# A two-layer CIN kernel: 64x32 tiles with single fields as weights meet 230 streaming products, in place of product rows that meet single fields

## The reference, cut to what matters

```python
B, M, D = 512, 39, 64                      # r_x: (512, 39, 64); W0: (39, 39, 128); W1: (39, 128, 128)
x0 = h = x
for W in (W0, W1):
    h = einsum('bid,bjd,ijh->bhd', x0, h, W)
    outs.append(h)
out = concatenate(outs, axis=1).sum(axis=-1)   # (512, 256)
```

## Time and profile before

| | |
|---|---|
| runs of the kernel | 349.57, 349.65, 349.71 us; median 349.65 |
| profiled execution, span from the first to the last instruction | 348.3 us (the profile holds no other time of this execution; the runs lie 1.3 us above the span) |
| setup, up to the first sums of the main loop | 0 to 104.8 us |
| main loop | 104.8 to 346 us |
| last copy and store | 2.3 us |
| busy share of PE, DVE, ACT, POOL | 94%, 49%, 33%, 3% |

### The profile page before, as it was taken

The page is one execution under the profiler, slowest core; times in us unless marked ns, Lnnn a source line. Parts: engine busy times, 40 slices in busy tenths (PEclk is TensorE's granted clock), DMA queues, the critical chain, the costliest instruction groups (busy, mean ns, idle before and its releaser), DMA issues.

```text
span 348.3 us, 11398 instructions
## 1 busy us (share of the span) xinstructions
PE 329.0 (94%) x5397; PEld 292.8 (84%) x5397; DVE 171.4 (49%) x212; ACT 114.7 (33%) x210; POOL 10.1 (3%) x14
## 2 busy tenths in 40 slices
PE   0899997999889999999999999999999999999997
PEld 0566664555779999998999999899999999999996
DVE  2205469467899385444536572635358090812000
ACT  1366653343542243060306214230522332142300
POOL 9200000000000000000000000000000000000000
PEclk9999999899999999999999999999999999999999
DMA  7950431300040003700000090000006000000000
GB/s 301 385 117 2 155 146 32 122 1 0 2 154 4 2 2 77 229 4 2 19 2 2 13 274 25 0 19 2 4 3 154 2 2 17 4 2 4 4 0 15
DMA packets 4350, 20.03 MB, mean 58 GB/s; under 512 B 592, under 2 KB 1104, under 8 KB 3920
## 3 DMA queue, kind: packets, MB, share of 16 engines
q1 hardware_dynamic: 3728, 18.79, 16.8%
q10 hardware_dynamic: 576, 0.52, 0.5%
HBM read 18.78 MB, written 0.52 MB: 55 GB/s over the span
## 4 chain that ended last, share of the span: by engine, by line
PE 90%; DVE 6%; DMA 1%; ACT 1%; issue 0%; SPq 0%; DVEq 0%
PE out_ps L545 37%; PE stage L511 32%; PE stage L473 8%; PE stage L487 7%; PE stage L493 4%; PE stage L476 2%; DVE arena L354 2%; DMA arena<-in_w_rows 1%; DVE arena L287 1%; DVE arena L400 1%; DVE arena L362 1%; DVE arena L359 1%; DVE arena L375 0%; ACT arena L423 0%; DVE arena L323 0%
## 5 line engine op out<-in xcount | busy, mean ns | idle before, releaser
L545 PE MATMUL out_ps<-arena 114*128 114x128 f32 (+2 forms) x968 | 128.7, 294 | 0.5 <-ACT arena L440 0.5
L511 PE MATMUL stage<-arena 128*60 128x80 f32 (+4 forms) x4096 | 126.2, 227 | 3.1 <-DVE arena L354 2.1
L511 PEld LDWEIGHTS stage<-arena 128*50 128x50 f32 (+2 forms) x4096 | 123.8, 128 | 5.3 <-issue 3.3
L545 PEld LDWEIGHTS out_ps<-arena 114*128 114x128 f32 (+1 forms) x968 | 121.7, 192 | 5.8 <-ACT arena L440 0.6
L440 ACT COPY arena<-stage 114x480 f32<-114x480 f32 (+4 forms) x136 | 72.5, 540 | 138.9 <-PE stage L511 138.9
L354 DVE TENSOR_TENSOR arena<-arena 128x3200 f32<-128x3200 f32 x16 | 55.7, 3486 | 28.4 <-PE stage L511 28.3
L473 PE MATMUL stage<-arena 128*128 128x380 f32 (+1 forms) x78 | 34.3, 523 | 10.1 <-DVE arena L289 10.1
L487 PE MATMUL stage<-arena 128*114 128x512 f32 (+1 forms) x60 | 31.5, 608 | 3.1 <-DVE arena L375 3.1
L357 DVE TENSOR_TENSOR arena<-arena 128x640 f32<-128x640 f32 x16 | 13.2, 824 | 39.2 <-PE stage L511 39.2
L362 DVE TENSOR_TENSOR arena<-arena 128x800 f32<-128x800 f32 x32 | 30.2, 985 | 0.0
L414 ACT COPY arena<-stage 128x480 f32<-128x480 f32 (+1 forms) x39 | 22.1, 568 | 22.5 <-PE stage L476 22.5
(11 more groups left out here) (22 smaller groups left out, 43.5 us busy)
## 6 DMA issues: line engine op xcount, KB each, us to landing
arena<-in_x_dense SPq DMA_DIRECT2D x8, 640.0 KB, 7.0
arena<-in_x_single SPq DMA_DIRECT2D x16, 320.0 KB, 5.0
arena<-in_c_first SPq DMA_DIRECT2D x1, 2560.0 KB, 9.1
arena<-in_w SPq DMA_DIRECT2D x2, 640.0 KB, 7.0
arena<-in_c_second SPq DMA_DIRECT2D x1, 1280.0 KB, 6.4
arena<-in_w SPq DMA_DIRECT2D x1, 1216.0 KB, 9.8
arena<-in_w_square SPq DMA_DIRECT2D x1, 800.0 KB, 4.3
arena<-in_c_one SPq DMA_DIRECT2D x2, 256.0 KB, 10.1
```

Of the source, the lines that this page charges most:

```text
L511: done = nc.tensor.matmul(bank[PART * part:PART * part + r1 - r0, 0:count * 2 * some] .rearrange("p (i b) -> p b i", b=2 * some)[:, 2 * (t ...
L545: done = nc.tensor.matmul(to, sums, w, start=tile == 0 and s == 0, stop=last, skip_group_check=True)
```

## The change

Setup and main loop are written anew; the mathematics is the same.

**Lists and tiles.** The products of a pair are now two lists of 230 (with field pairs of the first and of the second half of the fields, some copies of single fields for the remaining terms, and some extra pairs). They are the *streaming* operand. The stationary operand is 32 single fields (`ROWS`), of one sample: 64 rows by 32 columns of PE. A pair needs four such matmuls, sample (rows `r`) by list (`which`); even and odd pairs go to different halves of PE's columns (`odd`), so that 8 tiles of 64x32 take turns. No zeros are streamed. The two samples go to two PSUM banks; each list is cut in two halves of 115 `SLOTS`.

**ACT** empties a group of four pairs with four copies of 64 partitions and 460 elements (`L379`); half of them write to the other 64 partitions than they read.

**Weighing.** Eight batches of 32 pairs. 115 slots of all 128 rows, each with 64 samples as stationary columns and 128 columns of C, in turn in the two column halves, then 11 + 4 matmuls for the first layer's output; a quarter of it follows each unit of 8 pairs. ACT and DVE add the two halves at the end of a batch. The 4 use rows of the sums that SP gathers by DMA.

**POOL** copies the single fields among the products (two copies per unit).

**Setup.** 32 matmuls of 512 columns (`DIRECT`) give the part of C that W1 and the W0 of the pair give directly, with slots on the partitions. ACT copies each to SBUF and SP turns it with four DMAs from SBUF to SBUF: each reads 90 to 115 partitions, 512 bytes of each, and writes them in a row into *one* partition of `c0`. `c_landed` counts all 128. The rest of C comes from 845 matmuls of 32x128 (`mixed`, L420) in 29 PSUM banks, which DVE adds to `c0` (L345) once everything has landed. The first four units' products and sums lie between (`PRODUCTS_BEHIND`, `SUMS_BEHIND`).

The core of the diff:

```diff
-FIELDS = 39
-ONE = 39
+ROWS = 32
+ROW0 = (8, 0)
+LIST = 230
+SLOTS = 115
...
-    PAIRS = 64
-    HALF_PAIRS = PAIRS // 2
+    PAIRS = 32
+    UNIT = 8
+    GROUP = 4
+    B = 2 * PAIRS
...
+        DIRECT = [(g, which, q) for g in range(PLACES // 4) for which in range(2) for q in range(2)
+                  if 4 * g >= ROW0[which] and 4 * g + 4 <= ROW0[which] + ROWS]
...
+        COUPLES = [4, 6, 0]
+        def couple(g):
+            return g % 2 if g < BATCH_GROUPS else g % 3
+        SUMS_BEHIND = {16: 0, 20: 1, 24: 2, 28: 3}
+        PRODUCTS_BEHIND = {7: 0, 10: 1, 13: 2, 16: 3}
...
+        def _(pool):
+            nc.gpsimd.memset(view(c0, (1, ZEROED * HID)), 0.0).then_inc(c_zeroed, 1)
+            for u in range(UNITS):
+                x, to = x0 + u % X_RING * XU, prod0 + u % PROD_RING * PROD + LIST
+                pool.wait_ge(x_loaded[u % X_RING], 16 * (u // X_RING + 1))
+                if u < PROD_RING:
+                    pool.wait_ge(c_landed, C_LANDED)
+                    pool.wait_ge(out1_ready, 2)
+                else:
+                    pool.wait_ge(filled, 2 * (u - PROD_RING + 1))
+                T, TO = (X_WORDS, UNIT), (2 * LIST, UNIT)
+                nc.gpsimd.tensor_copy(view(to, TO, (1, COPY0)), view(x + X_MAIN + 21, T, (1, COPY0)))
+                nc.gpsimd.tensor_copy(view(to + SLOTS, TO, (1, COPY1)), view(x + X_MAIN + 29, T, (1, COPY1)))\
+                    .then_inc(copies_ready, 1)
...
+            for i, (g, which, q) in enumerate(DIRECT):
+                sp.wait_ge(direct_copied, i + 1)
+                j = direct_slots(g, which, q)
+                c = 2 * q + which
+                row = ROWS * c + 4 * g - ROW0[which]
+                for f in range(4):
+                    sp.dma_start(view(c0 + j * HID, (HID, SLOTS - j), (1, HID), rows=(row + f, row + f + 1)),
+                                 view(d0[c] + (4 * g - ROW0[which] + f) * HID, (1, HID), rows=(j, SLOTS)))\
+                        .then_inc(c_landed, 16)
...
+            def gather(n):
+                sp.wait_ge(emptied, BATCH_GROUPS * (n + 1))
...
+                for c in range(4):
+                    row = ROWS * c + ONE - ROW0[c % 2]
+                    sp.dma_start(view(t2_0 + (4 * (n % 2) + c) * B, (1, B), rows=(0, SLOTS)),
+                                 view(s0[n % 2], (B, SLOTS), (1, B), rows=(row, row + 1))).then_inc(t2_moved[n % 2], 16)
...
+            def products(u):
+                x, to = x0 + u % X_RING * XU, prod0 + u % PROD_RING * PROD
+                dve.wait_ge(x_loaded[u % X_RING], 16 * (u // X_RING + 1))
+                if u >= PROD_RING:
+                    dve.wait_ge(filled, 2 * (u - PROD_RING + 1))
+                T, TO = (X_WORDS, UNIT), (2 * LIST, UNIT)
+                second = to + LIST
+                main, half = x + X_MAIN, x + X_MAIN + 21
+                mult(view(to + 20, TO, (10, 20), (1, 10)), view(main, T, (1, 20), (0, 10)),
+                     view(x, T, (1, 20), (1, 10)), ALU.mult)
...
+                mult(view(second + 130, TO, (10, 10), (1, 10)), view(half + 9, T, (1, 10), (0, 10)),
+                     view(half + 9, T, (1, 10), (1, 10)), ALU.mult).then_inc(prod_ready, 1)
...
+            dve.wait_ge(c_landed, C_LANDED)
+            for k in range(MIXED):
+                words = min(IN_BANK, SLOTS - IN_BANK * k) * HID
+                c = view(c0 + k * BANK, (1, words))
+                dve.wait_ge(mixed_filled, k + 1)
+                add(c, c, bank_view(mixed_bank(k) * BANK, (1, words)), ALU.add).then_inc(c_added, 1)
+                if k in PRODUCTS_BEHIND:
+                    products(PRODUCTS_BEHIND[k])
...
+            act.wait_ge(c_landed, C_LANDED)
+            act.wait_ge(v_ready, 1)
+            for g in range(GROUPS):
+                n, in_batch = divmod(g, BATCH_GROUPS)
+                at = COUPLES[couple(g)] * BANK
+                act.wait_ge(filled, g + 1)
+                for odd in range(2):
+                    for q in range(2):
+                        done = nc.scalar.copy(
+                            view(s0[n % 2] + 8 * in_batch + 2 * odd, (1, 2), (B, SLOTS), (4, 2),
+                                 rows=(HALF * q, HALF * q + HALF)),
+                            bank_view(at + 2 * SLOTS * q, (BANK, 2), (2, SLOTS), (1, 2),
+                                      rows=(HALF * odd, HALF * odd + HALF)))
+                done.then_inc(emptied, 1)
...
+                nc.tensor.matmul(bank_view(i % DIRECT_BANKS * BANK, (1, 4 * HID), rows=(0, SLOTS)),
+                                 view(u0 + which * LIST + q * SLOTS, (1, SLOTS)),
+                                 view(w1_0 + 4 * g * HID, (1, 4 * HID)), start=True, stop=True).then_inc(direct_filled, 1)
+            def mixed(k):
+                bank = mixed_bank(k)
+                if k < 8:
+                    pe.wait_ge(direct_copied, len(DIRECT) - DIRECT_BANKS + k + 1)
+                else:
+                    pe.wait_ge(c_added, k - 8 + 1 if k < 12 else k - 4 + 1)
+                first = [True] * 4
+                for j in range(IN_BANK * k, min(IN_BANK * k + IN_BANK, SLOTS)):
+                    of = [terms(c % 2, PAIR_OF[c][j]) for c in range(4)]
+                    for t in range(2):
+                        for c in range(4):
+                            if t >= len(of[c]):
+                                continue
+                            row, m = of[c][t]
+                            done = nc.tensor.matmul(
+                                bank_view(bank * BANK + j % IN_BANK * HID, (1, HID), rows=(ROWS * c, ROWS * c + ROWS)),
+                                view(v0 + row * ROWS, (1, ROWS)), view(w1_0 + m * HID, (1, HID)),
+                                start=first[c], stop=True, skip_group_check=True)
+                            first[c] = False
+                done.then_inc(mixed_filled, 1)
...
-                for part, (r0, r1) in enumerate([(0, FIRST_PART[tile]), (FIRST_PART[tile], rows)]):
-                    done = nc.tensor.matmul(
-                        bank[PART * part:PART * part + r1 - r0, 0:count * 2 * some]
-                        .rearrange("p (i b) -> p b i", b=2 * some)[:, 2 * (t - t0):2 * (t - t0) + 2, :],
-                        view(prod0[(2 * p + hf) % PRODS] + in_unit * W_ROWS + r0, (1, r1 - r0)),
-                        view(single0 + t * SLOTS + first, (PAIRS * SLOTS, 2), (1, count)), start=True, stop=True)
+            def sums(g):
+                u, turn = divmod(g, 2)
+                before = last_user(g)
+                if before is not None:
+                    pe.wait_ge(emptied, before + 1)
+                else:
+                    pe.wait_ge(c_added, COUPLES[couple(g)] + 2 if g < BATCH_GROUPS else MIXED)
+                if turn == 0:
+                    pe.wait_ge(prod_ready, u + 1)
+                    pe.wait_ge(copies_ready, u + 1)
+                for m in range(2):
+                    for odd in range(2):
+                        pair = GROUP * turn + 2 * m + odd
+                        for r in range(2):
+                            rows = (HALF * r, HALF * r + HALF)
+                            for which in range(2):
+                                c = 2 * odd + which
+                                done = nc.tensor.matmul(
+                                    bank_view((COUPLES[couple(g)] + r) * BANK + m, (2, LIST),
+                                              rows=(ROWS * c, ROWS * c + ROWS)),
+                                    view(x0 + u % X_RING * XU + pair * X_WORDS + X_MAIN + ROW0[which], (1, ROWS), rows=rows),
+                                    view(prod0 + u % PROD_RING * PROD + pair * 2 * LIST + which * LIST, (1, LIST), rows=rows),
+                                    start=True, stop=True)
+                done.then_inc(filled, 1)
-                sums = view((s_x0 if tile % 2 else s_w0) + s * B, (1, B), rows=(0, rows))
...
-                done = nc.tensor.matmul(to, sums, w, start=tile == 0 and s == 0, stop=last, skip_group_check=True)
+            def weigh(n, turn):
+                at = (2 + n % 2) * BANK
+                if turn == 0:
+                    pe.wait_ge(emptied, BATCH_GROUPS * (n + 1))
+                each = -(-SLOTS // BATCH_UNITS)
+                for j in range(each * turn, min(each * turn + each, SLOTS)):
+                    side = j % 2
+                    rows = (HALF * side, HALF * side + HALF)
+                    sums_of = view(s0[n % 2] + j * B, (1, B))
+                    nc.tensor.matmul(bank_view(at + HID, (1, HID), rows=rows), sums_of, view(c0 + j * HID, (1, HID)),
+                                     start=j < 2, stop=True, skip_group_check=True)
+                if turn < BATCH_UNITS - 1:
+                    return
+                for j in range(CROSS):
+                    side = j % 2
+                    nc.tensor.matmul(bank_view(at, (1, HID), rows=(HALF * side, HALF * side + HALF)),
```

(27 more changed lines are left out.)

696 lines of the change are left out of this document (270 added, 426 removed).

## The result

The changed kernel takes **487.36 us** (median of 4 runs, 485.74 to 488.15), the kernel before 349.68 beside it (349.57 to 350.1): ratio 1.392, 95% interval 1.3888 to 1.3953. The forecast was 325 us, with a range up to 420.

A forecast was written before the change was run, and what follows sets the result against it. PE's work was taken to bound the kernel: landing 98 + to unit 4 50 + main loop 158 + last weighing 15 + end 3 = 324 us of span, 325 us measured-equivalent, 7% faster; likeliest case 308 to 345, range up to 420.

The forecast's parts named there:

- What bounds the kernel now: Whole old kernel: PE, busy 94% of the span, is the time; PE work left and setup delay to PE count.
- Sums, new: Main-loop sums on PE: a group of 4 pairs takes 0.85 us, nearly all eight tiles streaming at once.
- The rivals with four and two tiles at once: Main-loop sums: groups of 1.54 us give 369 us in all, 3.1 us give 500; chance 0.10 together.
- Weighing, new: Main-loop weighing on PE: column halves share time, a slot costs 0.111 us, a batch of 130 slots 14.4 us.
- ACT: ... 460 cost 0.54 ... eight are 3.5 us. PE stays the bound.: Main loop: ACT's copies of 460 elements cost 0.54 us, eight per unit 3.5 us, below PE's 5.65.
- DVE and POOL: Main-loop unit: DVE's products 4.1 us, POOL's two copies at most 1 us, together 5.1 of PE's 5.65.
- as long as PE's 5.65 us cover them: Main loop: copies, products and gathers cost nothing while hidden behind PE's 5.65 us per unit of 8 pairs.
- I take 2.8 on average ... `c_landed` at 98 us.: Setup transfers: 250 us serially, 2.8 blocks of partitions written at once on average, so 89 us, landing at 98.
- the transfers hold it up: Rival, setup: fewer than 2.2 blocks written at once, landing past 123 us, kernel slower (361 to 486 us); chance 0.27.
- At 0.5 that is 64 us: Setup lower bound: SP issues 128 transfers at 0.5 us each, 64 us, landing not before 75 us.
- the transfers hardly count: Rival, setup: only SP's issuing bounds the transfers, landing at 75 us, 302 us in all; chance 0.17.
- From there to unit 4, and the end: After the landing: 50 us to unit 4; at the finish, last batch's weighing 15 us and end 3 us.

The follow-up runs named there:

- b_late_out: Changed kernel with ACT's copies writing runs of four, plus ACT moving and DVE adding a batch's result later: 410.63 us (one run).
- c_rotate_half: Changed kernel with neighbouring transfers rotated over different blocks of 32 partitions and pieces of 256 bytes instead of 512: 432.16 us (one run).
- b_two_queues: On b_all, every other group of transfers is issued by ACT instead of SP: 343.92 us (4 runs), ratio 0.9829 to the kernel before.
- b_all: Changed kernel with ACT writing runs of four, b_late_out's later result, POOL's copies on DVE and rotated transfers: 358.05 us, ratio 1.0229.

## Why the prediction was wrong

**What bounds the kernel now**: nothing in the runs speaks against it, but what it led to, that the PE work left is the time, wasn't true of the new kernel: PE is busy for 276.5 us, and 207 us of standing still come beside it. The two large waits are for the transfers and for ACT's copies.

**Sums, new.** Right: 0.85 forecast, 0.89 us a group with the end of the last record (64 in 1.78), 0.86 up to the next work (352.13 to 353.85 in the trace). Eight tiles stream at once with hardly a loss. The rivals with four and two tiles at once (1.54, 3.1) fall, and so does the estimate of 1.16 that the prediction worked out from the Trainium skill's 10.6.

**Weighing, new.** Right: 0.111 forecast, 58 records in 3.4 to 3.5 us are 60 ns with the end of the last, 56 without it, 0.112 a slot.

**"ACT: ... 460 cost 0.54 ... eight are 3.5 us. PE stays the bound."** This is the step that failed in the main loop. A copy took 966 ns, 7.7 us for eight, more than PE's 5.65. The rows were of copies that write runs of at least 8 words; the new ones write lone words, in steps of 16 and 240 bytes. I priced the copy by its number of elements and never looked at its last dimension. The runs that show it: writes all side by side, in fours and in pairs take 537, 537 and 567 ns; reads side by side change nothing (968). So my price was right for the shape that it came from. The Trainium skill (Advanced Engine Details and Errata, SBUF Cachelines) says that SBUF has lines of 16 bytes and that two accesses to one line in a row are needed to hide the access time. By that rule these copies would be slow, and pairs as quick as fours; both agree with the runs, but for the 30 ns between pairs and fours.

**DVE and POOL.** DVE's 4.1 us was right (units follow one another in 4.1 us at 341.09 and 345.23). "two copies are at most 1 us" was wrong for POOL: the first of the two took 0.25 us alone, 8.9 to 18.8 in the changed kernel, and 25.5 in b_late_out, when it began while DVE multiplied without a pause. That hid behind ACT, then behind DVE's lateness, and showed once, in b_late_out. The third wait, DVE in `take_out` behind ACT's copies, I didn't see at all; it cost 17 us (427.5 against 410.6) once the copies were quick. With these three gone the period is 5.48 to 5.54 us. The 5.65 of the forecast was a good sum of PE's work, and what failed is the condition "as long as PE's 5.65 us cover them".

**The setup: "I take 2.8 on average ... `c_landed` at 98 us."** The other step that failed, in size and in its picture. 250 us of serial transfers ended at 174.4, by the same sum 1.5 blocks at once, not 2.8. The rival "the transfers hold it up" had the right mechanism (decides from 123 us on) with 0.27; with 1.5 blocks its sum would have been 361 + 40 = 401 us. Shown: the same transfers in an order that spreads them over the blocks need 120 us instead of 166, half the bytes 115, and all sixteen engines on each transfer gain nothing (176). So the place where the bytes are written bound them, as the earlier trace rows said for halves of the partitions: queued transfers to other blocks didn't help, and the drift of the queues on which I built did little. The Trainium skill ("SBUF — State Buffer", Door 1: The DMA port swizzle) names the port of a block; the order of the transfers mattered as it would by that rule, yet its serial sum of 243 us was not reached: some overlap there was.

**"At 0.5 that is 64 us"**: the lower bound was wrong too. The earlier trace rows showed loads of 0.40 to 0.64 us. Here an issue took 0.61 us at the least and 0.81 in the median in after, and 0.78 to 0.82 where nothing else bounds. The floor is some 105 us, and the rival "the transfers hardly count", 302 us at 0.17, was out of reach for 128 transfers issued by SP: by the issues alone the landing is at 13 + 106 = 119 us (c_rotate_half), only 4 us ahead of the break-even of 123, or 346 us by the prediction's own sum.

**From there to unit 4, and the end**: 50 and 18 us forecast, 50.1 and 18.6 measured.

**How the numbers follow.** The two unknowns were treated as the only ones. The range ended at 420 because no case added an engine's excess to late transfers; with only one of the two errors the time would have been 401 (325 + 76) or 408 (325 + 83), inside it. The repaired kernel bears the rest of the sum out: in b_two_queues the landing is at 118.6 us, 20.6 past the forecast 98, and the time of 343.92 is 19 above 325.

## What to carry to other kernels

Price a copy by a row with the same last dimension, not only the same count: two neighbours per step cost 567 ns where lone words cost 966. Before many small transfers between partitions are put on the start of a kernel, count them times an issue (here 0.8 us) as a floor, and order them so that neighbours in the queue write to different blocks. When PE's work shrinks, add up each other engine's unit anew with its worst rows, and look for whoever waits in program order behind it; the waits come out one behind the other, so one fix shows the next.

## What the runs showed of the hardware

- A copy of 460 elements by ACT from PSUM to SBUF that writes lone words (steps of 16 and 240 bytes) takes 966 ns; in pairs 567; in fours or all side by side 537.
- Eight tiles of 64x32 with 230 streaming columns: 28 ns a record with the end of the last of 64, against an estimated 193 for the columns of one.
- POOL's copy of 72 elements takes 0.24 us, or 8.9 to 25.5 us where it begins within an unbroken row of DVE's multiplications; then it ends when that row does. The Trainium skill ("SBUF — State Buffer", Who interferes with whom) has a DVE operation with two inputs in SBUF contend with GpSimd's reads; the rows agree. That it is this lock was not tried by itself.
- PE's granted clock fell to 0.50, the 1.2 GHz level, in the 124 us in which it did nothing; behind the idle 8.1 us at 345.41 the same 64 records took 3.33 us that took 1.78 a unit later.
- An issue of a transfer that turns rows into one partition takes SP 0.61 us at the least and 0.81 in the median; two issuing engines together took 106.7 us where one took 120.5 (b_all). Why it stops near 107 us with two stays open.
